# One ring of five PSUM banks and row-paired maxima products in an attention and feed-forward layer

## Chip, core and metric

One core of a Trainium2 chip runs the whole layer in one launch. The metric is the device time of a launch in microseconds (us); lower is better. The engines are TensorE (PE, with its weight loads as PEld), VectorE (DVE), ScalarE (ACT) and GpSimd (POOL); SyncE (SP) issues most of the DMAs. Each engine has its own written-out instruction stream, and semaphores alone order the streams against each other.

## What is computed

Input x and a context c, each 32 batches of 128 channels by 512 positions. Cut to what matters:

```python
x = x + xattn(layernorm(x), c)           # 8 heads of 16 channels, over 512 x 512 positions
x = x + ffn(layernorm(x))
# xattn: q = rope(Wq x + bq), k = rope(Wk c + bk), v = Wv c + bv
#        softmax(q k^T / 4) v, then Wo and bo
# ffn:   gate = bitlinear(x, w_gate); up = bitlinear(x, w_up)     (512 -> 2048)
#        y = fwht(silu(gate) * up); out = bitlinear(y, w_down)    (2048 -> 512)
# bitlinear: activations quantised to 8 bits by their row's absolute maximum, weights ternary
```

The softmax subtracts a maximum for each query. Any number near the true maximum serves, since it cancels between numerator and denominator.

## The kernel before

The work of one batch is spread over several steps. `step(t)` on every engine works on parts of batches t+2 to t-4 at once, and `for t in range(FIRST, LAST)` runs the steps. Inside `step` each engine's order is written out by hand, one call per piece of work, so an engine that waits holds back everything listed behind it.

Attention for a batch goes so:

- `project` makes q and k (f32, 128x512 each). DVE multiplies them with sine and cosine tables (`rope_sin`, `rope_cos`), SP moves the rotated half (`shift`, 2 DMAs), POOL adds (`turn`). Rows (channels) are ordered by channel first, then head, so that the rotated channels are the first 64 partitions.
- The result is cut into three bf16 parts whose sum is the f32 value: ACT makes part one and two (`first_part`, `second_part`), POOL the rests (`rest`, `third_part`). SP stacks them (`stack_part`, L314 to L329): 12 DMAs a batch write six blocks of 16 rows into `q_stack` and `k_stack`, in the pairings of `Q_TERMS` and `K_TERMS`, so that one product over 96 rows gives q k^T nearly to f32.
- `score_max` (L446 to L455): 32 products a batch, 96 rows deep, 128 queries by 512 keys, alternately into two banks `s1`. DVE takes each one's row maximum (`reduce_scores`, L1035). `max_transpose` turns the 128x32 maxima (L466), ACT negates them, and `stack_max` writes them as row 96 of `q_stack` by one DMA.
- `scores` (L470 to L481): 32 products again, now keys by queries and 97 rows deep, so that the maximum is already subtracted, alternately into two banks `s2`. ACT takes the exponential (`exps`, L726).
- `weigh` (L483 to L497): 8 groups a batch of four products each with v, 17 columns of weights for each head; the four write 32-partition strips of the bank `pv` side by side. In f32 the trace counts two instructions for each product, 8 in a group.
- After groups 3 and 7, `normalise` (L1037) transposes `pv` on DVE and takes the reciprocal of the sums; POOL multiplies (`mix`, L1314); after the second half DVE transposes back (`turn_back`), and `attn_out` is the product with Wo (L504).

Then the feed-forward part: `residual`, norm and quantisation on DVE and ACT; `gate_rows` (L522) and `xq_transpose` (L512); `gate_up` (8 groups of 16 products, L536) with `half_gates`, `tanh`, `glu` as consumers; the Walsh-Hadamard transform partly on POOL (`butterfly`) and partly as products (`hadamard`, L550); `y_transpose` (L561) and `down` (L574).

PSUM has eight banks: two `s1`, two `s2`, `pv`, and a ring of three. The names in `RING` take the ring's banks in turn in the order of the list, which is PE's order: `begin` waits until the bank's user before has been read, `end` tells that it is full.

Of the kernel before, what the change touches and what calls it, by code (L numbers as in the profile page):

```python
# [12 lines left out]
NH, DH = 8, 16  # L13
# [17 lines left out]
RING = {"yT0": 4, "yT1": 4, "down": 4, "wo": 2, "v": 0, "y0": 3, "mT": 1, "y1": 3, "y2": 3, "y3": 3, "hg": 2,  # L31
        "xqT": 2, "gate0": 2, "up0": 2, "gate1": 2, "up1": 2, "q": -1, "k": -1, "gate2": 2, "up2": 2, "gate3": 2,
        "up3": 2}
NRING = 3
# [5 lines left out]
FIRST, LAST = -6, B + 5  # L40

# [48 lines left out]
def layer(nc, x, ctx_in, proj_t, table_t, late_t, wg_t, wu_t, wd_t, out):  # L90
    stack = ExitStack()
    with stack:
# [83 lines left out]
        s1 = [stack.enter_context(nc.psum_tensor(f"s1_{i}", [128, 512], F32)) for i in range(2)]  # L176
# [42 lines left out]
        s1_full, s1_max = [sem(f"s1_full{i}") for i in range(2)], [sem(f"s1_max{i}") for i in range(2)]  # L219
# [77 lines left out]
        def _(sp):  # L297
# [16 lines left out]
            def stack_part(b, part):  # L314
                if not live(b):
                    return
                k = slot(b)
                sp.wait_ge((part1, part2, part3)[part], b + 1)
                sp.nop(nofuse=True)
                if part == 0:  # L320
                    wait(sp, s2_full, 32 * (b - 2))
                    sp.nop(nofuse=True)
                    if b < 3:
                        sp.wait_ge(ones_rows_set, b + 1)
                        sp.nop(nofuse=True)
                for w, (terms, dst) in enumerate(((Q_TERMS, q_stack[k]), (K_TERMS, k_stack[k]))):
                    for r in range(len(terms)):
                        if terms[r] == part:
                            sp.dma_start(dst[DH * r:DH * (r + 1), :, :], parts[:, part, w, :]).then_inc(stacked, 16)  # L329
# [14 lines left out]
            def stack_max(b):  # L344
# [4 lines left out]
                sp.dma_start(q_stack[slot(b)][STACK:STACK + 1, :, :], neg_max[:, :]).then_inc(max_stacked, 16)  # L349
# [20 lines left out]
            def step(t):  # L370
                load_late_consts(t + 1)
                load(t + 2)
                stack_max(t - 1)
                shift(t + 1)
                load_residual(t - 1)
                stack_part(t + 1, 0)
                stack_part(t + 1, 1)
                store(t - 4)
                stack_part(t + 1, 2)
                load_consts(t + 3)  # L380
# [7 lines left out]
        def _(pe):  # L388
# [57 lines left out]
            def score_max(b, n):  # L446
                if not live(b):
                    return
                k, p, i = slot(b), n % 2, n // 2
                h, c = 2 * (i // KC) + p, i % KC  # L450
                if n == 0:
                    pe.wait_ge(stacked, 16 * STACK_DMAS * (b + 1))
                wait(pe, s1_max[p], 16 * b + i)
                pe.matmul(s1[p][:, :], q_stack[k][0:STACK, h, 128 * c:128 * (c + 1)],  # L454
                          k_stack[k][0:STACK, h, :], start=True, stop=True).then_inc(s1_full[p], 1)  # L455

            def max_transpose(b):
# [5 lines left out]
                for p in range(2):  # L463
                    pe.wait_ge(s1_max[p], 16 * (b + 1))
# [5 lines left out]
            def scores(b, n):  # L470
# [4 lines left out]
                if n == 0:  # L475
                    pe.wait_ge(max_stacked, 16 * (b + 1))
# [3 lines left out]
                pe.matmul(s2[n % 2][:, :], k_stack[k][0:STACK + 1, h, 128 * c:128 * (c + 1)],  # L480
                          q_stack[k][0:STACK + 1, h, :], start=True, stop=True).then_inc(s2_full, 1)  # L481
# [96 lines left out]
            def step(t):  # L578
                bias_product(t)
                scores(t - 2, 19)  # L580
                score_max(t - 1, 16)
                weigh(t - 2, 3)
                score_max(t - 1, 17)
                scores(t - 2, 20)
                score_max(t - 1, 18)
                scores(t - 2, 21)
                y_transpose(t - 4, 0)
                score_max(t - 1, 19)
                scores(t - 2, 22)
                scores(t - 2, 23)  # L590
                score_max(t - 1, 20)
                weigh(t - 2, 4)
                scores(t - 2, 24)
                scores(t - 2, 25)
                score_max(t - 1, 21)
                score_max(t - 1, 22)
                weigh(t - 2, 5)
                score_max(t - 1, 23)
                scores(t - 2, 26)
                score_max(t - 1, 24)  # L600
                scores(t - 2, 27)
                y_transpose(t - 4, 1)
                score_max(t - 1, 25)
                scores(t - 2, 28)
                scores(t - 2, 29)
                score_max(t - 1, 26)
                down(t - 4, 0, 4)
                scores(t - 2, 30)
                up_sum(t - 1)
                score_max(t - 1, 27)  # L610
                score_max(t - 1, 28)
                scores(t - 2, 31)
                weigh(t - 2, 6)
                weigh(t - 2, 7)
                down(t - 4, 4, 8)
                score_max(t - 1, 29)
                score_max(t - 1, 30)
                down(t - 4, 8, 12)
                down(t - 4, 12, 16)
                score_max(t - 1, 31)  # L620
                attn_out(t - 2)
                project_v(t)
                hadamard(t - 3, 0)
                max_transpose(t - 1)
                score_max(t, 0)
                score_max(t, 1)
                hadamard(t - 3, 1)
                score_max(t, 2)
                hadamard(t - 3, 2)
                hadamard(t - 3, 3)  # L630
                score_max(t, 3)
                gate_rows(t - 2)
                xq_transpose(t - 2)
                scores(t - 1, 0)
                score_max(t, 4)
                scores(t - 1, 1)
                gate_up(t - 2, "gate", 0)
                gate_up(t - 2, "up", 0)
                scores(t - 1, 2)
                scores(t - 1, 3)  # L640
                gate_up(t - 2, "gate", 1)
                scores(t - 1, 4)
                gate_up(t - 2, "up", 1)
                scores(t - 1, 5)
                weigh(t - 1, 0)
                scores(t - 1, 6)
                scores(t - 1, 7)
                score_max(t, 5)
                project(t + 1, "q")
                score_max(t, 6)  # L650
                scores(t - 1, 8)
                score_max(t, 7)
                project(t + 1, "k")
                gate_up(t - 2, "gate", 2)
                scores(t - 1, 9)
                scores(t - 1, 10)
                score_max(t, 8)
                score_max(t, 9)
                weigh(t - 1, 1)
                scores(t - 1, 11)  # L660
                score_max(t, 10)
                scores(t - 1, 12)
                score_max(t, 11)
                gate_up(t - 2, "up", 2)
                scores(t - 1, 13)
                scores(t - 1, 14)
                gate_up(t - 2, "gate", 3)
                scores(t - 1, 15)
                score_max(t, 12)
                scores(t - 1, 16)  # L670
                weigh(t - 1, 2)
                score_max(t, 13)
                score_max(t, 14)
                scores(t - 1, 17)
                gate_up(t - 2, "up", 3)
                gate_sum(t + 1)
                score_max(t, 15)
                scores(t - 1, 18)
# [6 lines left out]
        def _(act):  # L685
# [169 lines left out]
            def max_out(b):  # L855
                if not live(b):
                    return
                wait(act, max_stacked, 16 * b)
# [4 lines left out]
            def step(t):  # L863
                norm1_apply(t + 1)
                exps(t - 1, 2)
                sign_piece(t - 2, 2, 4)
                exps(t - 1, 3)
                tanh(t - 2, 0)
                exps(t - 1, 4)
                tanh(t - 2, 1)  # L870
                exps(t - 1, 5)
                load_weights(t, 1, 1)
                abs_piece(t + 1, 0, 0)
                round_y(t - 3, 0)
                sign_piece(t - 2, 2, 5)
                abs_piece(t - 1, 2, 1)
                load_weights(t + 3, 0, 0)
                exps(t - 1, 6)
                exps(t - 1, 7)
                abs_piece(t - 1, 2, 2)  # L880
                exps(t - 1, 8)
                below_top(t - 3, 0)
                exps(t - 1, 9)
                exps(t - 1, 10)
                sign_piece(t - 2, 2, 6)
                round_y(t - 3, 1)
                sign_piece(t - 1, 1, 3)
                exps(t - 1, 11)
                abs_piece(t + 1, 0, 1)
                exps(t - 1, 12)  # L890
                exps(t - 1, 13)
                sign_piece(t, 0, 1)
                exps(t - 1, 14)
                sign_piece(t, 0, 2)
                abs_piece(t - 1, 2, 3)
                exps(t - 1, 15)
                tanh(t - 2, 2)
                abs_piece(t, 1, 0)
                abs_piece(t - 1, 2, 4)
                tanh(t - 2, 3)  # L900
                exps(t - 1, 16)
                abs_piece(t, 1, 1)
# [4 lines left out]
                below_top(t - 3, 1)  # L907
                exps(t - 1, 20)
                exps(t - 1, 21)
                exps(t - 1, 22)  # L910
                abs_piece(t + 1, 0, 2)
                exps(t - 1, 23)
                yT_out(t - 3, 0)
                abs_piece(t - 1, 2, 5)
                exps(t - 1, 24)
                second_part(t + 1)
                abs_piece(t + 1, 0, 3)
# [497 lines left out]
```

## Time and profile before

| what | value |
|---|---|
| median of 3 runs | 1508.82 us (1507.08 to 1510.89) |
| profiled execution | 1509.78 us, its span 1508.0 us |
| PE busy | 1414.5 us, 94% of the span |
| DVE busy | 1229.5 us, 82% |
| ACT busy | 1168.6 us, 77% |
| POOL busy | 1069.9 us, 71% |
| HBM over the span | 31 GB/s |

A matmul's busy time in the trace is longer than the time after which the next can start, since matmuls are pipelined: distances between starts say what PE can do. The chain of waits is followed back from the last instruction, and the durations in its pieces are such distances. The time before about 200 us is the loading and rounding of the weights and the filling of the pipeline; from about 1400 us the pipeline empties.

### The profile page before, as it was taken

To read this page: it belongs to the slowest core of one execution; us is meant where nothing else is said; L and a number is where in the kernel's file an instruction comes from. 1 tells how busy PE (TensorE), PEld (TensorE's weight loads), DVE (VectorE), ACT (ScalarE), POOL (GpSimd) and SP (SyncE) were. 2 spreads that over 40 slices of the span, in tenths; PEclk is the share of its full clock that TensorE was granted. 3 is DMA by queue.
4 is the path that set the end of the run, shared out by engine and by line. 5 is a ranking of instruction groups with operands and counts; after the bars stand their busy time and mean duration, and the time that the engine had idled before them with its cause. 6 is when DMAs were issued, how large, how long until landed. Compare 5 with 4: busy or idle time off the path is not lost.

```text
span 1508.0 us, 31029 instructions
## 1 busy us (share of the span) xinstructions
PE 1414.5 (94%) x11042; PEld 743.4 (49%) x11042; DVE 1229.5 (82%) x2149; ACT 1168.6 (77%) x2033; POOL 1069.9 (71%) x803
## 2 busy tenths in 40 slices
PE   2678999999999999999999999999999999999985
PEld 1214455455555544555555445555555455555443
DVE  2757788888888888888888888988888888888744
ACT  4586778888788888887788788877887888877663
POOL 3122788777777788777777887777778877777662
PEclk9677999999999999999999999999999999999998
DMA  8852344333344443323434433323344433333000
GB/s 211 225 116 46 58 72 77 62 65 62 61 74 68 78 78 64 66 62 60 77 64 78 78 64 71 60 64 69 64 78 78 72 64 63 64 52 64 16 8 15
DMA packets 81113, 108.13 MB, mean 72 GB/s; under 512 B 9664, under 2 KB 59200, under 8 KB 79936
## 3 DMA queue, kind: packets, MB, share of 16 engines
q1 hardware_dynamic: 77744, 93.56, 34.6%
q10 hardware_dynamic: 3216, 12.58, 2.4%
q8 instruction: 89, 1.46, 0.5%
q14 instruction: 64, 0.52, 0.2%
HBM read 38.73 MB, written 8.39 MB: 31 GB/s over the span
## 4 chain that ended last, share of the span: by engine, by line
PE 79%; ACT 9%; DVE 4%; DMA 3%; issue 3%; SPq 1%; POOL 1%; POOLq 0%; ACTq 0%; DVEq 0%
PE pv L495 15%; PE ring L536 14%; PE s L480 13%; PE s L454 13%; PE ring L574 7%; PE ring L550 6%; PE ring L428 4%; ACT region L726 4%; PE ring L504 2%; PE ring L442 2%; DMA region<-parts 2%; PE ring L561 1%; ACT parts L821 1%; ACT xqT L735 1%; ACT y_last L769 1%
## 5 line engine op out<-in xcount | busy, mean ns | idle before, releaser
L1035 DVE TENSOR_REDUCE maxima<-s 128x1 bf16<-128x512 f32 x1024 | 671.1, 683 | 110.4 <-PE s L454 107.8
L726 ACT ACTIVATE region<-s 128x512 f32<-128x512 f32 x1024 | 570.4, 594 | 101.0 <-PE s L480 93.0
L454 PE MATMUL s<-region 96*128 96x512 bf16 x1024 | 369.3, 390 | 26.2 <-DVE maxima L1035 13.5
L1293 POOL TENSOR_TENSOR region<-region,th 128x512 f32<-128x512 f32 x126 | 158.9, 1273 | 293.8 <-DVE th L1130 292.1
L480 PE MATMUL s<-region 97*128 97x512 bf16 x1024 | 357.8, 384 | 7.6 <-ACT region L726 4.0
L495 PE MATMUL pv<-region,v_ext 128*17 128x512 f32 x2048 | 264.2, 599 | 0.0
L292 POOL TENSOR_TENSOR region<-region 128x512 f32<-128x512 f32 x189 | 240.6, 1273 | 12.5
L293 POOL TENSOR_TENSOR region<-region 128x512 f32<-128x512 f32 x189 | 241.1, 1275 | 0.0
L454 PEld LDWEIGHTS s<-region 96*128 96x128 bf16 x1024 | 95.0, 98 | 207.3 <-DVE maxima L1035 110.9
L480 PEld LDWEIGHTS s<-region 97*128 97x128 bf16 x1024 | 91.0, 98 | 172.7 <-ACT region L726 140.0
L290 POOL TENSOR_TENSOR region<-region 128x1024 f32<-128x1024 f32 x63 | 148.0, 2371 | 3.4 <-DVE region L293 3.4
L536 PEld LDWEIGHTS ring<-xqT,wg 128*128 128x128 bf16 x2048 | 123.3, 98 | 52.6 <-issue 33.7
L536 PE MATMUL ring<-xqT,wg 128*128 128x128 bf16 x2048 | 135.8, 219 | 6.5 <-ACT xqT L735 1.7
L550 PE MATMUL ring<-late_const,region 128*128 128x128 f32 x1024 | 131.5, 277 | 7.5 <-POOL region L290 5.6
L536 PE MATMUL ring<-xqT,wu 128*128 128x128 bf16 x2048 | 135.3, 219 | 0.1
L550 PEld LDWEIGHTS ring<-late_const,region 128*128 128x128 f32 x1024 | 127.7, 194 | 15.1 <-issue 5.7
L536 PEld LDWEIGHTS ring<-xqT,wu 128*128 128x128 bf16 x2048 | 123.7, 98 | 15.2 <-DVE region L1121 0.3
L574 PE MATMUL ring<-wd,y_last 128*128 128x512 bf16 x512 | 128.1, 385 | 0.8 <-ACT y_last L787 0.8
L1121 DVE TENSOR_TENSOR region<-ring,half_gate 128x512 f32<-128x512 f32 x128 | 87.5, 684 | 41.8 <-PE ring L536 41.2
L836 ACT ACTIVATE v_ext<-ring 128x512 f32<-128x512 f32 x32 | 19.1, 598 | 126.9 <-PE ring L442 126.9
L1331 POOL TENSOR_TENSOR region<-region,rope_c 64x1024 f32<-64x1024 f32 x32 | 75.6, 2362 | 29.6 <-DMA rope_c<-region 27.4
L495 PEld LDWEIGHTS pv<-region,v_ext 128*17 128x17 f32 x2048 | 36.9, 95 | 109.8 <-issue 75.1
(111 smaller groups left out, 1862.5 us busy)
## 6 DMA issues: line engine op xcount, KB each, us to landing
region<-parts SPq DMA_DIRECT2D x384, 128.0 KB, 4.3
x_in<-in_x SPq DMA_DIRECT2D x32, 256.0 KB, 2.7
c_in<-in_ctx SPq DMA_DIRECT2D x32, 256.0 KB, 3.0
rope_c<-region SPq DMA_DIRECT2D x64, 128.0 KB, 2.3
x_res<-in_x SPq DMA_DIRECT2D x32, 256.0 KB, 2.9
out<-o_sb SPq DMA_DIRECT2D x32, 256.0 KB, 4.7
region<-in_wg_t ACTq DMA_DIRECT2D x1, 2048.0 KB, 8.9
region<-in_wu_t ACTq DMA_DIRECT2D x1, 2048.0 KB, 7.6
```

Of the source, the lines that this page charges most:

```text
L290: return engine.tensor_tensor(o[:, :, half, :], a[:, :, 0, :], a[:, :, 1, :], ALU.subtract if half else ALU.add)
L292: engine.tensor_tensor(o[:, :, 0, :], a[:, :, 0, :], a[:, :, 1, :], ALU.add)
L293: return engine.tensor_tensor(o[:, :, 1, :], a[:, :, 0, :], a[:, :, 1, :], ALU.subtract)
L454: pe.matmul(s1[p][:, :], q_stack[k][0:STACK, h, 128 * c:128 * (c + 1)], k_stack[k][0:STACK, h, :], start=True, stop=True).then_inc(s1_full ...
L480: pe.matmul(s2[n % 2][:, :], k_stack[k][0:STACK + 1, h, 128 * c:128 * (c + 1)], q_stack[k][0:STACK + 1, h, :], start=True, stop=True).then ...
L495: last = pe.matmul(pv[32 * i:32 * i + DH + 1, :], v_ext[b % 2][:, c, 4 * g + i, :], probs[:, (4 * u + i) % 8, :], start=(c == 0), stop=(c ...
L536: last = pe.matmul(bank(f"{name}{j}")[:, 128 * i:128 * (i + 1)], w[:, c, o:o + 128], xqT[:, c, :], start=(c == 0), stop=(c == HC - 1), ski ...
L550: last = pe.matmul(bank(f"y{j}")[:, 128 * c:128 * (c + 1)], z[:, o:o + 128], had[:, :], start=True, stop=True, skip_group_check=True)
L574: last = pe.matmul(bank("down")[:, :], yqT[:, c, :], wd[:, c, :], start=(c == 0), stop=(c == IC - 1))
L726: act.activation(probs[:, n % 8, :], s2[n % 2][:, :], ACT.Exp, scale=SCALE).then_inc(exp_done, 1)
L1035: dve.reduce_max(maxima[:, c, h:h + 1], s1[p][:, :], AXX).then_inc(s1_max[p], 1)
L1293: pool.tensor_tensor(zj, zj, th[:, j % 2, :], ALU.mult).then_inc(glu_done, 1)
```

## The change

1. **Ring.** `s1` is gone; the ring has five banks and takes the maxima products too, as `m0` to `m31`. `s2` and `pv` stay as they are. `RING` follows the new order of PE.
2. **Rows.** Channels are now ordered so that heads 0 to 3 lie in partitions 0 to 63 and heads 4 to 7 in 64 to 127 (with the rotated channels in every second block of 16). The stacks of the two head groups lie at different rows: terms 0 to 3 at rows 0 to 63 and 64 to 127. Terms 4 and 5 of the second group lie at rows 32 to 63, its row of maxima at row 31, and rows 0 to 30 of `q_stack` are set to zero once.
3. **Maxima products.** `score_max` issues two products, one of each head group, over the four main terms alone: 64 rows each, rows 0 to 63 and rows 64 to 127, into two ring banks. 16 such pairs a batch stand for the 32 products of before. The two smallest terms are left out of the maxima, not of the scores.
4. **Scores.** The products of heads 4 to 7 are 128 rows deep where they were 97.
5. **DMAs.** Every stacking DMA is cut in two by head group (24 a batch for 12), so is the one of the maxima (2 for 1); `shift` has 4 for 2, and `rope_sin` and `turn` work on 128 partitions for 64.
6. **Mix** goes from POOL to DVE, into `normalise`.
7. **Orders** of PE, ACT, DVE and SP are written anew, with the start of a step at another place.

```diff
-STACK_DMAS = 2 * len(Q_TERMS)
-SHIFTS = 2
-RING = {"yT0": 4, "yT1": 4, "down": 4, "wo": 2, "v": 0, "y0": 3, "mT": 1, ...
-NRING = 3
+STACK_DMAS = 4 * len(Q_TERMS)
+SHIFTS = 4
+RING = {"k": -1, "m4": 0, "m5": 0, "m6": 0, "m7": 0, "m8": 0, "m9": 0, "up2": 2, "m10": 0, "m11": 0, "gate3": 2,
+        "m12": 0, "m13": 0, "m14": 0, "m15": 0, "up3": 2, "m16": 0, "m17": 0, "m18": 0, "m19": 0, "yT0": 3, "m20":
+        0, "m21": 0, "m22": 0, "m23": 0, "m24": 0, "m25": 0, "m26": 0, "m27": 0, "m28": 0, "m29": 0, "m30": 0,
+        "m31": 0, "down": 3, "yT1": 3, "mT": 0, "wo": 1, "v": -1, "y0": 2, "y1": 2, "y2": 2, "m0": -1, "m1": -1,
+        "y3": 2, "hg": 1, "xqT": 1, "gate0": 1, "up0": 1, "gate1": 1, "q": -2, "up1": 1, "gate2": 1, "m2": -1, "m3":
+        -1}
+NRING = 5
+MAX_ROW = (STACK, 31)
+ROWS = (slice(0, STACK + 1), slice(0, 128))
+MAIN = (slice(0, 4 * DH), slice(4 * DH, 8 * DH))
+HALF = NH // 2
+def term_rows(g, r):
+    lo = DH * r if g == 0 else 64 + DH * r if r < 4 else 32 + DH * (r - 4)
+    return slice(lo, lo + DH)
+def heads(g):
+    return slice(HALF * g, HALF * (g + 1))
...
             def step(t):       # SP, the new order
+                stack_part(t, 2)
+                load(t + 2)
+                store(t - 4)
+                load_residual(t - 1)
+                load_consts(t + 3)
+                shift(t + 1)
+                load_late_consts(t + 1)
+                stack_part(t + 1, 0)
+                stack_part(t + 1, 1)
+                stack_max(t)
...
-            def score_max(b, n):
...
-                wait(pe, s1_max[p], 16 * b + i)
-                pe.matmul(s1[p][:, :], q_stack[k][0:STACK, h, 128 * c:128 * (c + 1)],
-                          k_stack[k][0:STACK, h, :], start=True, stop=True).then_inc(s1_full[p], 1)
+            def score_max(b, i):
...
+                k, c = slot(b), i % KC
+                if i == 0:
+                    pe.wait_ge(stacked, 16 * STACK_DMAS * (b + 1))
+                for g in range(2):
+                    begin(f"m{2 * i + g}", b)
+                for g in range(2):
+                    h = HALF * g + i // KC
+                    end(f"m{2 * i + g}",
+                        pe.matmul(bank(f"m{2 * i + g}")[:, :], q_stack[k][MAIN[g], h, 128 * c:128 * (c + 1)],
+                                  k_stack[k][MAIN[g], h, :], start=True, stop=True))
...
+                rows = ROWS[h // HALF]
+                pe.matmul(s2[n % 2][:, :], k_stack[k][rows, h, 128 * c:128 * (c + 1)], q_stack[k][rows, h, :],
+                          start=True, stop=True).then_inc(s2_full, 1)
...
-                dve.wait_ge(s1_full[p], 16 * b + i + 1)
-                dve.reduce_max(maxima[:, c, h:h + 1], s1[p][:, :], AXX).then_inc(s1_max[p], 1)
+                full(dve, f"m{n}", b)
+                free(f"m{n}", dve.reduce_max(maxima[:, c, h:h + 1], bank(f"m{n}")[:, :], AXX))
...
                 dve.reciprocal(inv_sum[:, :], blocks[:, :, DH]).then_inc(inv_done, 1)
+                dve.wait_ge(inv_done, 2 * b + g + 1)
+                if g == 0:
+                    wait(dve, attn_done, b)
+                dve.tensor_tensor(mixed[:, :].rearrange("p (n g e) -> p n g e", g=2, e=DH)[:, :, g, :],
+                                  blocks[:, :, 0:DH], inv_sum[:, :].unsqueeze(2).to_broadcast([128, 16, DH]),
+                                  ALU.mult).then_inc(mixed_done, 1)
```

PE's new order, written short (sc = `scores`, M = `score_max`, one pair each, W = `weigh`; a plus marks the batch one later): project k+; W0; sc 8, 9; M2; W1; M3; sc 10; M4; sc 11; up 2; sc 12; M5; sc 13; gate 3; sc 14, 15; M6; W2; M7; sc 16, 17; up 3; sc 18, 19; M8; W3; sc 20, 21; M9; y_transpose 0; sc 22, 23; W4; M10; sc 24, 25; M11, M12; sc 26, 27; W5; sc 28, 29; M13; W6; sc 30; M14, M15; sc 31; down (4 products); y_transpose 1; W7; max_transpose; down (12); attn_out; project_v; sc+ 0; hadamard 0; sc+ 1; hadamard 1, 2; M+ 0; hadamard 3; gate_rows; sc+ 2; xq_transpose; sc+ 3; gate 0; up 0; sc+ 4; gate 1; sc+ 5; project q; up 1; sc+ 6; gate 2; sc+ 7; M+ 1.

On ACT, `first_part` stands behind `exps` 17 as before, `second_part` behind `exps` 27 (it stood behind 24), and `max_out` behind the second `yT_out`. On DVE, maxima 23 to 31, `normalise` 1 and `turn_back` stand ahead of `residual`, and `quantise` between maximum 1 and the first `half_gates`. POOL keeps its order, without `mix`.

## Rows read from the trace of the kernel before

**Rows 1.** The page, part 1: busy us (share), instructions, by engine.
```profile
PE 1414.5 (94%) x11042; PEld 743.4 (49%) x11042; DVE 1229.5 (82%) x2149; ACT 1168.6 (77%) x2033; POOL 1069.9 (71%) x803
```

**Rows 2.** Stretches: span, busy of PE, PEld, DVE, ACT, POOL, PEclk, DMA, GB/s.
```profile
500.00:700.00 200.00, 198.92 (x1600) 106.37 (x1600) 173.60 (x309) 161.89 (x290) 153.34 (x115) 1.00 0.40 71
700.00:900.00 200.00, 199.16 (x1592) 102.73 (x1589) 174.55 (x305) 165.41 (x292) 160.67 (x121) 1.00 0.40 70
```

**Rows 3.** Chain of waits, 765 to 819 us: start, us to the next piece, what.
```profile
765.02 0.45 PE ring L561 x8
...
773.29 1.03 PE ring L504 x2
...
809.02 0.22 PE s L454
809.24 0.86 PE ring L574 x4
...
810.32 0.43 PE s L454 x2
...
810.97 1.84 PE pv L495 x16
...
816.16 1.02 PE ring L504 x2
...
818.97 0.32 PE ring L466 x4
819.29 0.54 PE s L454 x2
```

**Rows 4.** The same chain around one single group of weigh, then at xqT.
```profile
803.97 0.98 PE pv L495 x8
804.96 0.54 PE s L480 x2
...
823.78 0.60 ACT xqT L735
824.38 0.14 issue
824.52 1.95 PE ring L536 x32
```

**Rows 5.** Groups by line, 700 to 1000 us: count | busy us, mean ns | idle before.
```profile
L454 PEld LDWEIGHTS s<-region 96*128 96x128 bf16 x224 | 20.7, 97 | 35.4 <-DVE maxima L1035 16.8 <-issue 6.0
L1321 POOL TENSOR_TENSOR mixed<-turned_pv,inv_sum 128x256 f32<-128x256 f32 x14 | 8.7, 621 | 0.5
L1130 DVE SCALAR_TENSOR_TENSOR th<-th,ring 128x512 f32<-128x512 f32 x28 | 19.1, 682 | 0.4
L1099 DVE TENSOR_SCALAR gate_diag<-late_const,sc,w_half 128x128 f32<-128x128 f32 x7 | 2.4, 336 | 0.0
L821 ACT ACTIVATE parts<-region 128x1024 bf16<-128x1024 f32 x7 | 7.4, 1057 | 0.0
```

**Rows 6.** PE in order of time: start, us, what, count.
```profile
800.09 0.38 PE L454 MATMUL s<-region 96*128 96x512 bf16 x1
...
816.09 1.10 PE L504 MATMUL ring<-attn,late_const 128*128 128x512 f32 x2
819.22 0.61 PE L454 MATMUL s<-region 96*128 96x512 bf16 x2
```

**Rows 7.** DVE and ACT in order of time, attention's end to quantised x.
```profile
817.33 0.75 DVE L1066 SCALAR_TENSOR_TENSOR h_res<-ring,out_bias,x_res 128x512 f32<-128x512 f32 x1
822.69 0.43 DVE L1107 TENSOR_SCALAR xq<-turned_pv 128x512 bf16<-128x512 f32 x1
842.16 1.06 ACT L821 ACTIVATE parts<-region 128x1024 bf16<-128x1024 f32 x1
```

**Rows 8.** POOL and SP's queue in order of time: start, us to the last issue's end.
```profile
812.11 2.14 POOL L1344 TENSOR_TENSOR parts<-rope_c,parts 128x1024 bf16<-128x1024 f32 x1
814.32 1.19 SPq L329 DMA_DIRECT2D region<-parts  x2
821.07 0.72 SPq L349 DMA_DIRECT2D region<-neg_max  x1
843.36 4.08 SPq L329 DMA_DIRECT2D region<-parts  x6
```

**Rows 9.** DMA issues of 814 to 816 us: KB each, us to landing.
```profile
region<-parts SPq DMA_DIRECT2D x2, 128.0 KB, 3.4
```

More of the change, by code:

```diff
@@ L593, in step @@
[L593 to L627, printed above, removed]
+                project(t + 1, "k")
+                weigh(t - 1, 0)
+                scores(t - 1, 8)
+                scores(t - 1, 9)
                 score_max(t, 2)
-                hadamard(t - 3, 2)
-                hadamard(t - 3, 3)
+                weigh(t - 1, 1)
@@ L631, in step @@
                 score_max(t, 3)
-                gate_rows(t - 2)
-                xq_transpose(t - 2)
-                scores(t - 1, 0)
+                scores(t - 1, 10)
                 score_max(t, 4)
[L636 to L647, printed above, removed]
+                scores(t - 1, 11)
+                gate_up(t - 2, "up", 2)
+                scores(t - 1, 12)
                 score_max(t, 5)
-                project(t + 1, "q")
+                scores(t - 1, 13)
+                gate_up(t - 2, "gate", 3)
+                scores(t - 1, 14)
+                scores(t - 1, 15)
                 score_max(t, 6)
-                scores(t - 1, 8)
+                gate_sum(t + 1)
@@ L652, in step @@
+                weigh(t - 1, 2)
                 score_max(t, 7)
[L653 to L665, printed above, removed]
@@ new lines, in step @@
+                scores(t - 1, 19)
+                score_max(t, 8)
+                weigh(t - 1, 3)
+                scores(t - 1, 20)
+                scores(t - 1, 21)
+                score_max(t, 9)
+                y_transpose(t - 3, 0)
+                scores(t - 1, 22)
+                scores(t - 1, 23)
+                weigh(t - 1, 4)
+                score_max(t, 10)
+                scores(t - 1, 24)
+                scores(t - 1, 25)
+                score_max(t, 11)
+                score_max(t, 12)
@@ new lines, in step @@
+                scores(t - 1, 26)
+                scores(t - 1, 27)
+                weigh(t - 1, 5)
+                scores(t - 1, 28)
+                scores(t - 1, 29)
+                score_max(t, 13)
+                weigh(t - 1, 6)
+                scores(t - 1, 30)
+                score_max(t, 14)
+                score_max(t, 15)
+                scores(t - 1, 31)
+                down(t - 3, 0, 4)
+                y_transpose(t - 3, 1)
+                weigh(t - 1, 7)
+                max_transpose(t)
@@ new lines, in step @@
+                up_sum(t)
+                down(t - 3, 4, 8)
+                down(t - 3, 8, 12)
+                down(t - 3, 12, 16)
+                attn_out(t - 1)
+                project_v(t + 1)
+                scores(t, 0)
+                hadamard(t - 2, 0)
+                scores(t, 1)
+                hadamard(t - 2, 1)
+                hadamard(t - 2, 2)
+                score_max(t + 1, 0)
+                hadamard(t - 2, 3)
+                gate_rows(t - 1)
+                scores(t, 2)
@@ L680, in _ @@
+                xq_transpose(t - 1)
+                scores(t, 3)
+                gate_up(t - 1, "gate", 0)
+                gate_up(t - 1, "up", 0)
+                scores(t, 4)
+                gate_up(t - 1, "gate", 1)
+                scores(t, 5)
+                project(t + 2, "q")
+                gate_up(t - 1, "up", 1)
+                scores(t, 6)
+                gate_up(t - 1, "gate", 2)
+                scores(t, 7)
+                score_max(t + 1, 1)
             for t in range(FIRST, LAST):
@@ L1374, in _layout @@
     half = ROPE // 2
-    rows = [(d, h) for d in range(DH) for h in range(NH)]
+    order = [d for q in (0, 2, 1, 3) for d in range(half * q, half * (q + 1))]
+    rows = [(d, h) for g in range(2) for d in order for h in range(HALF * g, HALF * (g + 1))]
     perm = np.array([DH * h + d for d, h in rows])
```

269 lines of the change are left out of this document (112 added, 157 removed).

## The prediction

> **What bounds the kernel now.** I read the engines' totals first [rows 1]: PE 94%, DVE 82%, ACT 77%, POOL 71%. A PE share says little by itself, so the table of stretches comes next [rows 2]: in the steady part PE is busy 99.6% of the time (199.16 of 200 us) at full granted clock, DVE 87%, ACT 83%, POOL 80%. Third, the chain of waits: the two pieces of L504 (`attn_out`) stand 816.16 - 773.29 = 42.87 us apart, and nearly all pieces between them are PE's own [rows 3]. So a batch costs 42.87 us, 32 batches 1372 us, and the other 136 us of the span are weights, filling and emptying. PE's instruction distances are the bound.
>
> Those distances: one score product 0.22 us, two 0.43, so 0.218 each [rows 3]. One group of `weigh` takes 0.98, two adjacent ones 1.84, so a group is 0.86 and 0.12 more goes once for an excursion; the two score products right behind it take 0.54 instead of 0.43, another 0.11 [rows 3, 4]. The same shows without any four-fold packing: the four transposes of the maxima (8 columns of weights) take 0.32 where eight full transposes take 0.45, that is 0.10 too much, and the two products behind them again take 0.54 [rows 3]. I read this as the price of changing the shape in which the array is used: about 0.11 us for every change, the length of a weight load (97 ns [rows 5]) that isn't hidden. In PE's order of before there are 16 changes a batch (seven excursions to `weigh`, one to `max_transpose`).
>
> The Trainium skill says the same of the cause: TensorEngine Tiling (Array Packing), section Key Properties, has it that changing the tiling mode, not just the tile, drains the engine. The rows agree for column tiles at 0.11 us; no row shows a row tile. By that rule the isolated pairs would be nearly worthless, which is what I cost below.
>
> **The change, part by part.** *Maxima products.* 32 products of 0.218 go: 6.98 us a batch. 16 pairs come. If the two halves of the array run side by side, a pair takes 0.218 plus the offset of the second. That offset isn't in the trace: from 0 (four `weigh` products in 0.86 us leave nearly none) to 0.10 (a whole weight load [rows 5]). I take 0.03, nearer to `weigh`: 16 x 0.248 = 3.97. Saved: 3.0 us a batch; bounds 1.9 to 3.5.
>
> *Changes of shape.* I counted them in PE's new order, a pair as a third shape: 37 a batch, because only M11/M12 and M14/M15 are adjacent, and seven borders lie directly between a pair and a `weigh`. That is 21 more. At 0.11: +2.3 us. Bounds: 21 borders lie between pairs and full-array products alone; if a row pair changes for free, the others are 16, as before, and the term is 0. On the other side 0.16 each (L454's duration of 0.38 us [rows 6] less its distance of 0.218) would give 21 x 0.16 = 3.4. I take 2.3, since two kinds of change in the trace have one price.
>
> The net on PE is 3.0 - 2.3 = 0.7 us less a batch. Deeper scores (128 rows for 97) cost nothing: four 128-row products of `down` take 0.86, 0.215 each, as 96 rows do [rows 3].
>
> *From attention's end to the gates.* L504 starts at 816.09, DVE's residual at 817.33, the quantised x at 822.69, xqT is copied out from 823.78, and gates start at 824.52 [rows 4, 6, 7]: 8.4 us, of which PE waits about 0.7 (0.60 copy and 0.14 issue behind a transpose). In the new order PE has between the two: attn_out 1.0, v 0.9, four hadamards 3.6, four scores 0.9, one pair 0.45 with its changes, gate_rows 0.4, transposes 0.3 = 7.5 us. The same as before (one pair and four scores stand where six single products, one score and max_transpose stood). One DVE maximum between residual and absmax is gone, 0.3 us off that chain at best. I take no change; bounds -0.3 to +0.5.
>
> *Mix on DVE.* The 128x256 product of two SBUF operands isn't on DVE in the trace. Below, 0.34 (128x128, L1099); above, 0.68 (128x512, L1130) [rows 5]; I take 0.45 and 0.1 for the wait behind the reciprocal: 2 x 0.55 = 1.1 us. DVE then has 174.55/200 x 42.87 = 37.4, plus 1.1 = 38.5 of 42.2 us. It hides as long as PE's batch is over about 40 us. On the path to attn_out it replaces 0.62 us on POOL and a hand-over [rows 5]; from W7's end the chain is transpose, reciprocal, mix, transpose, some 2.4 us, and PE has max_transpose and twelve of `down` (2.9 us) to cover it. POOL gets 1.2 us shorter: nothing, it had slack. Wider `rope_sin` and `turn`: more partitions, same columns, nothing.
>
> *Ring.* With five banks PE waits for the fifth user back. Going down the new order with DVE at 0.6 to 0.65 us a maximum I find each bank free before its next user: closest are M12 and M15 (within 0.3 us) and max_transpose, which waits for maximum 31. Before, single maxima products also waited now and then (16.8 us in 300, on the weight load's row [rows 5]), with little effect on PE. I take 0; bounds -0.3 to +0.8.
>
> *DMAs.* A stacking issue takes SP 0.6 to 0.68 us (six in 4.08, two in 1.19), though the 8 KB of the maxima takes 0.72 [rows 8]: the size hardly matters, so cut DMAs cost their number. SP goes from 12 x 0.65 to 24 x 0.65 = 15.6 us, and about 22 us in all: no bound by itself. But the path matters: first_part ends 843.22 [rows 7]; then come 12 + 8 issues (13.0), two of maxima (1.4) and, because `stack_part(t, 2)` now stands behind `stack_max`, the last four (2.6); with the last one's landing (3.4 from its issue [rows 9], so 2.8 more) that is 19.8 us. The product that waits for it, M+ 0, is due at 819.22 + 42.87 = 862.09 in the old order [rows 6], 18.9 us after first_part, and in the new one 1.9 later (two hadamards and two scores more ahead of it, max_transpose less): 20.8. Waits for second_part and max_out on the way are worth 0 to 2 us. So it arrives between 1.0 early and 1.0 late. Halved DMAs should land sooner than 3.4; I take 0; upper bound 1.2.
>
> *Sum.* 32 x 0.7 = 22 us off the profiled execution's 1509.8 (span 1508.0 and 1.8 around it) is 1487; filling and emptying I leave alone, +-8. The median of before is 1 us under that execution. I say **1488**.
>
> **Rivals.**
> *B, row changes are cheap.* The 21 borders of pairs with full products cost nothing: PE would be 3.0 shorter, 39.9, and DVE with 38.5 and its own waits becomes the joint bound; I give 40.5: 32 x 2.4 = 77 off, 1433. For it: no row shows that a row pair drains the array. Against: two kinds of change cost the same.
> The page TensorE: Matmul & The Clock Gate of the Trainium skill, section Part 3: Packing small matmuls, says that weight loads overlap running matmuls when the row groups differ. No run here shows it; it would speak for B.
>
> *C, the last stacking DMAs come late* (slower). M+ 0 waits at SP's queue; PE and everything behind it, gate_rows and the quantised x too, shift by the lateness, so nothing absorbs it. At 1.2 us late the net is +0.5 a batch: 1526. It decides from 0.7 us late. For it: 26 issues in one row on SP, the path has no more than 1 us of air. Against: smaller DMAs. A ring wait of 1.2 us would read the same in time.
>
> *D, the pairs don't overlap* (or their price is far higher): 3.5 comes back, 32 x 2.5 = 80 more, 1590. Against: four column tiles of `weigh` clearly overlap.
>
> *E, nothing left:* offset 0.06 and 0.12 a change: within 5 us of 1509.
>
> **How the numbers follow.** Forecast 0.44 (its own range 1472 to 1504), B 0.16, C 0.25, D 0.04, E 0.11. A tenth of the forecast's cases fall within 0.3% (4.5 us, what measuring can tell from no change), some of C's too. Faster 0.57, same 0.13, slower 0.30. The range reaches from B to C: 1428 to 1534.
>
> **What would show it.** The batch distance of L504 falls to about 42.2 us. From the start of a full product ahead of an isolated pair to the start of the one behind it about 0.69 us; near 0.47 instead means B. Adjacent pairs (M11, M12) about 0.25 each. PE stays over 98% busy in the steady stretch, DVE near 91%. `mixed` on DVE 0.4 to 0.5 us, its wait for PE not longer than before. No wait of L454's line on the stacking DMAs; 0.7 us or more a batch there is C. Wrong would I be if the chain shows ACT or DVE as its largest owner, or if PE's weight loads wait for ring banks over 1 us a batch.

## The result, and the profile after

The changed kernel takes 1549.68 us (median of 4 runs, 1546.31 to 1551.89) against 1509.86 us: ratio 1.026, 95% interval 1.023 to 1.029. It is 2.6% slower where I forecast 1.4% faster. The profiled execution took 1546.31 us, span 1544.5 us.

The page after: span, totals by engine, the owners of the chain, and three of its groups (count | busy us, mean ns | idle before).

```profile
span 1544.5 us, 32084 instructions
...
PE 1372.3 (89%) x11042; PEld 692.7 (45%) x11042; DVE 1325.6 (86%) x2213; ACT 1178.1 (76%) x2033; POOL 1050.6 (68%) x742
...
DVE 44%; PE 38%; issue 7%; ACT 7%; SPq 1%; DMA 1%; POOL 1%; ACTq 0%; DVEq 0%; POOLq 0%
...
L1049 DVE TENSOR_REDUCE maxima<-ring 128x1 bf16<-128x512 f32 x1024 | 638.6, 682 | 23.4 <-PE ring L482 23.0
...
L482 PE MATMUL ring<-region 64*128 64x512 bf16 x1024 | 197.9, 392 | 34.6 <-DVE maxima L1049 27.8
...
L1066 DVE TENSOR_TENSOR mixed<-turned_pv,inv_sum 128x256 f32<-128x256 f32 x64 | 111.4, 1741 | 2.2
```

PE fell from 94% to 89% busy [rows 1], and the chain of waits, 79% PE's before, belongs to DVE for 44%, which I had named as a sign of being wrong. The last line is the finding: mix on VectorE lasts 1.74 us on average where I had taken 0.45. The stretch that answers to [rows 2] (span, busy of PE, PEld, DVE, ACT, POOL, PEclk, DMA, GB/s):

```profile
700.00:900.00 200.00, 188.16 (x1567) 97.89 (x1565) 182.86 (x310) 157.60 (x279) 142.72 (x103) 1.00 0.24 74
```

PE is busy 94.1% instead of 99.6, at the same full clock; DVE 91.4% instead of 87.3.

The chain of waits around attention's end (start, us, what), to be held against [rows 3, 4]:

```profile
785.26 1.03 PE pv L525 x8
786.32 0.73 DVE turned_pv L1059
787.07 0.27 DVE inv_sum L1062
787.36 2.06 DVE mixed L1066
789.46 0.05 issue
789.51 0.72 DVE attn L1075
790.23 0.14 issue
790.36 1.11 PE ring L534 x2
...
834.57 1.11 PE ring L534 x2
```

The two pieces of `attn_out` are 44.21 us apart (42.87 before). Between W7 and `attn_out` no PE piece stands in the chain: the twelve products of `down` are over, and PE waits for `attn`. The list of waits over 300 us, seven batches, has it first, and a second wait at the maxima products (engine, line waited for: us in total, times, longest):

```profile
PE ring L534 <- DVE attn L1075: 7.9, 7, 1.1
PE ring L482 <- DVE maxima L1049: 4.3, 13, 0.4
```


What holds the mix shows when DVE's rows are laid beside POOL's (start, us, engine, what). First a mix while POOL is idle, in the filling of the pipeline, then the two of one batch:

```profile
113.16 2.13 POOL L1355 TENSOR_TENSOR parts<-rope_c,parts 128x1024 bf16<-128x1024 f32 x1 [5.52 <-ACT parts L841]
...
118.31 0.42 DVE L1066 TENSOR_TENSOR mixed<-turned_pv,inv_sum 128x256 f32<-128x256 f32 x1
...
818.87 2.14 POOL L1349 TENSOR_TENSOR rope_c<-region,parts 128x1024 f32<-128x1024 f32 x1
819.68 1.60 DVE L1066 TENSOR_TENSOR mixed<-turned_pv,inv_sum 128x256 f32<-128x256 f32 x1
820.96 1.46 POOL L312 TENSOR_TENSOR region<-region 128x512 f32<-128x512 f32 x1
...
830.97 4.86 POOL L310 TENSOR_TENSOR region<-region 128x1024 f32<-128x1024 f32 x2
831.57 2.04 DVE L1066 TENSOR_TENSOR mixed<-turned_pv,inv_sum 128x256 f32<-128x256 f32 x1
```

Alone the mix takes 0.42. Beside L1349, which ends at 821.01, it ends at 821.28; beside the first half of the L310 pair it ends at 833.61, just after that instruction. Its recorded duration is mostly standing still. All 64 mixes of this trace say the same: one starts while POOL is idle and takes 0.42 us; the other 63 start during a POOL instruction, and each ends 0.28 us after that instruction's end. POOL pays too: L312 behind it takes 1.46 where it takes 1.27 otherwise. This reading is what the experiments put to the test.

### The profile page after: what moved, and what is told of

Its sections match the earlier page's. It is cut to its first block, busy times and chain, and to the rows that moved or that the text cites. A ratio compares the mean times of both kernels' runs of the same rounds, so it can differ in the third digit from the quotient of the medians.

```text
span 1544.5 us, 32084 instructions
## 1 busy us (share of the span) xinstructions
PE 1372.3 (89%) x11042; PEld 692.7 (45%) x11042; DVE 1325.6 (86%) x2213; ACT 1178.1 (76%) x2033; POOL 1050.6 (68%) x742
## 4 chain that ended last, share of the span: by engine, by line
DVE 44%; PE 38%; issue 7%; ACT 7%; SPq 1%; DMA 1%; POOL 1%; ACTq 0%; DVEq 0%; POOLq 0%
DVE maxima L1049 18%; PE ring L566 10%; DVE mixed L1066 7%; PE pv L525 7%; PE s L510 6%; PE ring L452 4%; PE ring L482 4%; DVE turned_pv L1059 3%; PE ring L534 2%; DVE th L1150 2%; PE ring L604 2%; DVE region L1029 2%; DVE attn L1075 1%; DVE region L1038 1%; DVE region L1141 1%
## 5 line engine op out<-in xcount | busy, mean ns | idle before, releaser
L740 ACT ACTIVATE region<-s 128x512 f32<-128x512 f32 x1024 | 570.3, 596 | 138.7 <-PE s L510 136.6
L1049 DVE TENSOR_REDUCE maxima<-ring 128x1 bf16<-128x512 f32 x1024 | 638.6, 682 | 23.4 <-PE ring L482 23.0
L510 PE MATMUL s<-region 128*128 128x512 bf16 (+1 forms) x1024 | 355.0, 387 | 9.5 <-DMA region<-neg_max 6.6
L525 PE MATMUL pv<-region,v_ext 128*17 128x512 f32 x2048 | 269.5, 598 | 1.6 <-ACT region L740 1.6
L312 POOL TENSOR_TENSOR region<-region 128x512 f32<-128x512 f32 x189 | 245.9, 1301 | 13.1 <-ACT wd L729 0.6
L313 POOL TENSOR_TENSOR region<-region 128x512 f32<-128x512 f32 x189 | 241.0, 1275 | 0.0
L482 PE MATMUL ring<-region 64*128 64x512 bf16 x1024 | 197.9, 392 | 34.6 <-DVE maxima L1049 27.8
L510 PEld LDWEIGHTS s<-region 128*128 128x128 bf16 (+1 forms) x1024 | 86.7, 97 | 205.0 <-ACT region L740 124.9
L310 POOL TENSOR_TENSOR region<-region 128x1024 f32<-128x1024 f32 x63 | 153.2, 2451 | 3.5 <-DVE region L313 3.4
L482 PEld LDWEIGHTS ring<-region 64*128 64x128 bf16 x1024 | 49.0, 93 | 233.6 <-issue 181.2
L1066 DVE TENSOR_TENSOR mixed<-turned_pv,inv_sum 128x256 f32<-128x256 f32 x64 | 111.4, 1741 | 2.2
L1342 POOL TENSOR_TENSOR region<-region,rope_c 128x1024 f32<-128x1024 f32 x32 | 75.5, 2360 | 40.6 <-DMA rope_c<-region 38.4
```

Source lines behind the costliest of these rows:

```text
L312: engine.tensor_tensor(o[:, :, 0, :], a[:, :, 0, :], a[:, :, 1, :], ALU.add)
L313: return engine.tensor_tensor(o[:, :, 1, :], a[:, :, 0, :], a[:, :, 1, :], ALU.subtract)
L482: pe.matmul(bank(f"m{2 * i + g}")[:, :], q_stack[k][MAIN[g], h, 128 * c:128 * (c + 1)], k_stack[k][MAIN[g], h, :], start=True, stop=True))
L510: pe.matmul(s2[n % 2][:, :], k_stack[k][rows, h, 128 * c:128 * (c + 1)], q_stack[k][rows, h, :], start=True, stop=True).then_inc(s2_full, 1)
L525: last = pe.matmul(pv[32 * i:32 * i + DH + 1, :], v_ext[b % 2][:, c, 4 * g + i, :], probs[:, (4 * u + i) % 8, :], start=(c == 0), stop=(c ...
L740: act.activation(probs[:, n % 8, :], s2[n % 2][:, :], ACT.Exp, scale=SCALE).then_inc(exp_done, 1)
```

## Experiments

Two theories were put to the test. Theory 1: a VectorE instruction with both inputs in SBUF doesn't run beside a GpSimd instruction that reads SBUF; the two mixes lost the time, everything else came out as forecast. Theory 2: row pairs, the ring or the cut DMAs lost it, and the mix only sits on the chain because PE is late. Every kernel ran beside the kernel before on the same chip (its median 1509 to 1511 us); not all ran on one chip, so a difference between two of them is uncertain by about 2 us more.

| kernel | us, median | ratio to before, 95% | batch distance us |
|---|---|---|---|
| kernel before | 1509.9 | | 42.92 |
| changed kernel | 1549.7 | 1.023 to 1.029 | 44.27 |
| mix_on_pool | 1501.8 | 0.993 to 0.996 | 42.64 |
| inverse_in_psum | 1492.2 | 0.987 to 0.990 | 42.34 |
| slow_first_half | 1520.9 | 1.005 to 1.009 | 43.40 |
| slow_second_half | 1541.6 | 1.019 to 1.023 | 44.17 |
| full_depth_maxima | 1518.3 | 1.004 to 1.008 | 43.23 |
| fewer_changes | 1519.4 | 1.005 to 1.008 | 43.22 |
| two_moves | 1497.8 | 0.991 to 0.994 | 42.56 |
| old_mix_dve | 1584.3 | 1.047 to 1.052 | 45.3 |
| old_mix_dve_psum | 1536.4 | 1.017 to 1.020 | 43.74 |
| old_extra_dve | 1514.2 | 1.001 to 1.004 | 43.00 |

The batch distance is worked out from the starts of the first and last `attn_out` products between 400 and 1300 us, as in this answer on its line in the changed kernel (min/median/max ns, first and last start us):

```profile
L534 PE MATMUL ring<-attn,late_const x40: 592/630/668, 436.6 to 1278.1; 128*128 128x512 f32 x40
```

Two instructions a batch, 0.43 us apart: (1278.1 - 0.43 - 436.6)/19 = 44.27. Where I say below how much a wait grew per batch, the distances between the starts of PE's products in the traces were summed by kind over the same 19 or 20 batches and compared between two kernels; such a sum also holds the part of a wait that lies within a product's recorded duration, which the lists of waits leave out.

**mix_on_pool**: the changed kernel, mix undone.

```diff
-                dve.tensor_tensor(mixed[...][:, :, g, :], blocks[:, :, 0:DH], inv_sum..., ALU.mult)   # in normalise
+                mix(t - 1, 0)          # POOL's step, L1321's code of before
                 third_part(t + 1)
+                mix(t - 1, 1)
```

> The changed kernel with one edit undone: mix goes back to GpSimd (the second half behind third_part, as in the kernel before). Theory 1 (the mix on VectorE is what cost the time: each of its 64 instructions lasts 1.7 us instead of 0.43 because it stands still while a GpSimd instruction runs, and it delays attn_out and loads VectorE): the batch distance of attn_out falls from 44.2 to 42.4-42.8 us, the time to 1485-1505 us; VectorE still waits for GpSimd between the halves since turn_back stands right behind normalise, which may cost up to 0.7 us a batch, 1520 at most. Theory 2 (the row pairs, the ring of five or the cut DMAs lose the time, the mix only sits on the chain because PE is late): the time stays at 1535-1550 us and attn_out moves little.

1501.8 us: theory 1's range, and theory 2's 1535 to 1550 is out. All else of the change is still in this kernel, and together it is faster than before.

**inverse_in_psum**: only the place of one operand of mix is changed, and with it what PE waits for before it writes `pv` again.

```diff
-        inv_sum = sb("inv_sum", [128, 16], F32)
+        inv_sum = pv[:, 0:16]
...
-                    wait(pe, pv_turned, 2 * b + g)
+                    wait(pe, mixed_done, 2 * b + g)
```

> The changed kernel with mix on VectorE as it is, but the 16 columns of inv_sum lie in PSUM (the first columns of the pv bank) instead of SBUF, and PE waits for mix instead of for the transpose before it writes pv again. Same instructions, same engine; only one operand's memory is changed. Theory 1 (a VectorE instruction with two SBUF inputs and a GpSimd instruction exclude each other): mixed takes 0.40-0.55 us in all of its 64 instructions, the batch distance is 42.3-42.6 us, the time 1482-1498 us, close to what I had forecast. Theory 1b (mix is slow by its strided and broadcast operands in the steady part): mixed stays at 1.6-2.0 us and the time at 1545. Theory 2 (pairs, ring, DMAs): mixed gets short, but the time stays over 1530 us.

1492.2 us, 1.1% faster than before (ratio 0.989, 0.987 to 0.990). The mix's own line, all 64 of them (min/median/max ns):

```profile
L1066 DVE TENSOR_TENSOR mixed<-turned_pv,pv x64: 420/420/421, 107.1 to 1433.0; 128x256 f32<-128x256 f32 x64
```

and the same line in the changed kernel:

```profile
L1066 DVE TENSOR_TENSOR mixed<-turned_pv,inv_sum x64: 425/1628/2487, 107.5 to 1487.0; 128x256 f32<-128x256 f32 x64
```

The strides and the broadcast are the same, so they aren't what was slow (theory 1b of the expectation falls). One of the two inputs moved from SBUF to PSUM, and every wait beside POOL is gone. The Trainium skill states it: SBUF — State Buffer, section Who interferes with whom, says that a DVE instruction with two SBUF inputs contends with a GpSimd instruction that reads SBUF, and that the port pair they share is an exclusive lock. The traces agree, 0.42 against up to 2.49 us.

The distances between PE's starts say where the changed kernel's 1.93 us a batch over this one lie: 1.31 in front of `attn_out`, 0.71 at M11 and M12, and 0.1 less elsewhere. So both waits come from the mix, and nothing of note is left over.

**slow_first_half, slow_second_half**: `inverse_in_psum` with the inverse of one half of the heads in SBUF again.

```diff
-        inv_sum = pv[:, 0:16]
+        inverse = [pv[:, 0:16], pv[:, 0:16]]
+        inverse[0] = sb("inv_sum", [128, 16], F32)      # the other kernel: inverse[1]
```

> As inverse_in_psum, but for the first half of the heads the inverse lies in SBUF again, so only the first mix of a batch can be held by GpSimd. Theory 1: the first mix takes 1.2-1.8 us, the second 0.42. It loads VectorE with about 1.2 us more a batch in a stretch where maxima follow one on another; in the changed kernel PE waited 0.65 us a batch at M11 and M12 behind it. Expected distance 42.6-43.1 us, time 1500-1520 us. Theory 2 (only the path to attn_out counts): no change from 1492 us.

> As inverse_in_psum, but for the second half of the heads the inverse lies in SBUF again. Theory 1: the second mix takes 1.7-2.1 us, stands between attention's last product and attn_out, and PE waits about 1.1 us there: distance 43.3-43.5 us, time 1522-1532 us. If the two halves add up, slow_first_half and slow_second_half together lose the 57 us between 1492 and 1549.

1520.9 and 1541.6 us: 29 and 49 us more, where both halves slow lose 57. They don't add, and both came out above their range. The second mixes (median here 2.42 us, 2.03 in the changed kernel, since they meet the GpSimd instruction earlier) make PE wait up to 1.5 us for `attn`, 1.7 a batch by the starts. For the first, the waits (over 300 us, as above) name a cause that the changed kernel doesn't have:

```profile
PEld pv L526 <- DVE mixed L1067: 9.0, 7, 1.3
PE pv L526 <- DVE mixed L1067: 6.9, 7, 1.0
```

In this family PE may write `pv` only after the mix, for the inverse lies in it, so a slow first mix holds W4: 1.06 us a batch by the starts, all that this kernel loses. M11 and M12, where the changed kernel waits, don't wait longer here. The two kernels therefore show that either slow mix can cost PE time, but not the shares of the changed kernel; those are the 1.31 and 0.71 above.

**full_depth_maxima**: `inverse_in_psum` with the pairs' products at full depth (`FULL`: rows 0 to 95 for heads 0 to 3, all 128 for heads 4 to 7), order and all else kept.

```diff
-                        pe.matmul(bank(f"m{2 * i + g}")[:, :], q_stack[k][MAIN[g], h, 128 * c:128 * (c + 1)],
-                                  k_stack[k][MAIN[g], h, :], start=True, stop=True))
+                        pe.matmul(bank(f"m{2 * i + g}")[:, :], q_stack[k][FULL[g], h, 128 * c:128 * (c + 1)],
+                                  k_stack[k][FULL[g], h, :], start=True, stop=True))
```

> As inverse_in_psum, but each maxima product runs over the full array's rows (96 for heads 0-3, 128 for heads 4-7, so row 31 with an old maximum shifts the maxima of heads 4-7: the numbers that come out are others) instead of a 64-row pair; orders, ring, DMAs and all else stay. Theory 1 with my costing (a pair takes 0.22 us, each change of shape 0.105-0.11): 32 x 0.218 for 16 x 0.22 is +3.5 us, 21 changes fewer is -2.3 us: +1.2 us a batch, 43.2-43.6 us, 1520-1533 us. If row changes were free (a pair then saves all of its 0.22): +3.5 us, 1590 or more. If pairs are worthless: 1485-1495 us.

1518.3 us, 0.9 us a batch more than with pairs: somewhat under the expected 1.2, the distance just inside its range (43.2 to 43.6) and the time just under. So the pairs are worth about 0.9 us a batch net, not the 3.5 that 16 hidden products would be. Here is where the rest goes, in the chain of `inverse_in_psum` (start, us to the next piece, what):

```profile
740.37 0.32 PE ring L482 x2
740.69 0.32 PE s L510
741.01 0.32 PE ring L482 x2
741.33 0.32 PE s L510
...
746.37 0.54 PE s L510 x2
...
757.97 0.54 PE ring L482 x4
```

A single product takes 0.22 [rows 3]; one ahead of a pair takes 0.32. A pair takes 0.22 + 0.10, two adjacent pairs (M14, M15) 0.54, so a pair itself costs as much as one product, its second half next to nothing (it starts 3 ns behind the first), and each change of shape 0.10, close to the price read off `weigh` [rows 3, 4]. From the product ahead of an isolated pair to the one behind it are 0.64 us, where I had named 0.69 for my forecast and 0.47 for rival B: the pair with its two changes takes 0.42, as long as two single products. Summed over a batch by the starts, `full_depth_maxima` spends 3.3 us more on the 16 products that a pair hides (3.5, less a wait of 0.2 at M12); the pairs' 21 borders with full products cost 2.0, the f32 products behind a pair 0.2, and 0.2 goes elsewhere: 0.9 is left.

**fewer_changes, two_moves**: pieces of PE's order moved so that changes go.

```diff
+                score_max(t, 4)            # both kernels: M4 behind M3
                 scores(t - 1, 10)
-                score_max(t, 4)
...
+                score_max(t, 9)            # both: M9 behind W3
                 scores(t - 1, 20)
                 scores(t - 1, 21)
-                score_max(t, 9)
...
-                weigh(t - 1, 5)            # fewer_changes only
                 scores(t - 1, 28)
                 scores(t - 1, 29)
+                weigh(t - 1, 5)
```

> As inverse_in_psum, with three moves in PE's order that leave the ring's order as it is: M4 directly behind M3, M9 directly behind W3, scores 28 and 29 ahead of W5 instead of behind it. 4 changes of shape a batch fewer. Theory 1 (PE bound, 0.105-0.11 us for each change): -0.43 us a batch, 41.85 us, 1476-1482 us. If the earlier pairs or scores run into a wait on VectorE's maxima or ScalarE's exponentials, less: up to 1492 us.

1519.4 us: a clear miss, 27 us slower than `inverse_in_psum` where I expected it faster. Its chain:

```profile
766.71 0.34 PE s L510
767.05 0.02 issue
767.07 1.09 ACT region L740 x2
768.17 0.05 issue
768.21 0.39 PE s L510
768.60 0.98 PE pv L525 x8
```

Scores 28 and 29 go into the two `s2` banks and wait for exponentials 26 and 27 (the piece L740 x2); W5 behind them starts late, and exponential 28 waits for it (ACT for PE, 0.6 us), since it writes the probability tile that W5 reads.

> As fewer_changes, without its third move (scores 28 and 29 stay behind W5): M4 directly behind M3, M9 directly behind W3, 3 changes of shape a batch fewer than inverse_in_psum. If fewer_changes was lost by its third move alone (scores 28 and 29 waited for exponentials 26 and 27, and exponential 28 for W5 to free its place in the 8 probability tiles), the distance is 42.28 - 0.32 = 41.96 us and the time 1480-1486 us. If the shorter PE order runs into VectorE or ScalarE anyway: 1488-1496 us.

1497.8 us, 0.4% slower than `inverse_in_psum` and not 0.6% faster, above both stated ranges: the second miss. Three changes went, and this came:

```profile
752.33 0.34 PE s L510
752.70 0.04 issue
752.75 1.09 ACT region L740 x2
753.84 0.05 issue
753.89 0.39 PE s L510
```

The scores after M9 come one pair later, so PE stands at the next of them until two exponentials are done. PE is 98% busy in this order and ACT empties its two score banks one after the other, so a move that saves 0.1 us for PE can cost more in a wait for ACT: counting changes alone doesn't price a move.

**old_mix_dve, old_mix_dve_psum, old_extra_dve**: the part done alone in the kernel before.

```diff
                 dve.reciprocal(inv_sum[:, :], blocks[:, :, DH]).then_inc(inv_done, 1)
+                dve.wait_ge(inv_done, 2 * b + g + 1)                       # the first two
+                ...
+                dve.tensor_tensor(mixed[...], blocks[:, :, 0:DH], inv_sum..., ALU.mult).then_inc(mixed_done, 1)
...
+                wait(dve, extra_done, 2 * b + g)                           # old_extra_dve instead
+                dve.reduce_max(scratch[:, :], table_const[:, 0:256], AXX).then_inc(extra_done, 1)
```

> The kernel before with mix alone moved to VectorE (both operands in SBUF): one part of the change done alone. Theory 1: mixed takes 1.2-2.5 us there too; VectorE has some 5.5 us of air in a batch, the two mixes take 2.6 us of it beyond their own price, and the second delays turn_back by up to 1 us, where PE has little cover: 1512-1535 us. If the mix had its own price of 0.43 us and nothing else, the time would stay at 1505-1512 us. Theory 2: 1505-1512 us whatever mixed takes.

1584.3 us, 4.9% slower, twice as much as the whole change and far over my range. The mix alone (mean 1.38 us) hits the old order harder: in 300 us of the steady part the maxima's weight loads waited 30.7 us for DVE's maxima (16.8 before [rows 5]), and `attn_out` up to 0.9 us. By the starts, PE lost 2.4 us a batch, 1.4 around the score and maxima products and 1.0 in front of `attn_out`.

> The kernel before with mix on VectorE and inv_sum in PSUM. Theory 1: mixed 0.40-0.55 us; time 1503-1512 us, no difference from before. Theory 1b: mixed as long as in the version with both operands in SBUF, and the same time as that.

1536.4 us where I expected 1503 to 1512, with mix at 0.42 us throughout. Theory 1's price for the mix held, its consequence here didn't. The waits show PE's next `weigh` behind the mix in all 7 batches:

```profile
PEld pv L495 <- DVE mixed L1052: 7.3, 7, 1.1
```

That is `pv`, released after reciprocal and mix instead of after the transpose. By the starts this holds the weigh groups 0.6 us a batch longer, and `attn_out` comes 0.2 later; together they are the 0.82 us by which the batch grew. `old_extra_dve` takes the same DVE time without that wait and without POOL:

> The kernel before, mix on GpSimd as it was, with one more VectorE instruction of about 0.41 us (a row maximum over 256 constant columns, one SBUF input, its result is not used) right behind each reciprocal: the load of a short mix on VectorE without mix's wait for GpSimd and without a later release of pv. If VectorE's load alone is harmless in the old order: 1506-1514 us, and the 27 us that old_mix_dve_psum lost come from PE waiting for mix before it may write pv (1.1 us a batch in its trace). If the load itself or the later maxima cost them: 1525-1540 us.

1514.2 us (ratio 1.002, 1.001 to 1.004): 0.4 us of DVE twice a batch costs nearly nothing, as I had costed it. So DVE's load isn't what cost the 27 us; some three quarters of them are the later release of `pv`, by the starts, though a kernel with that wait alone was not run. In the new order the same wait is 0.2 us a batch, which fits that the PSUM operand pays there and not here.

## Why the prediction was wrong

The step that failed is **Mix on DVE**: "I take 0.45 and 0.1 for the wait behind the reciprocal: 2 x 0.55 = 1.1 us" and "from W7's end the chain is transpose, reciprocal, mix, transpose, some 2.4 us". The bounds, 0.34 and 0.68, came from VectorE rows that each read one tensor from SBUF; mix reads two. Measured: 0.42 of its own, but 1.6 us beside `rest` and 2.03 us beside `butterfly`, 3.6 us a batch in place of 0.9. POOL is busy 80% of the steady part [rows 2], and 63 of the 64 mixes met one of its instructions. The chain from W7's end (786.32 to 790.36) is 4.0 us, and PE's cover of 2.9 us didn't reach: 1.3 us a batch by the starts. The same excess puts DVE behind in the run of maxima, and PE waits 0.7 us a batch longer at M11 and M12. Instead of hiding, the term cost 44.27 - 42.34 = 1.9 us a batch, 57 us in all; no rival of mine named it. I had weighed VectorE's load, not what its instruction shares with POOL's.

The other steps, one by one:

- *Maxima products.* 3.0 us forecast with 0.03 for the second half of a pair; the offset is 3 ns and the term 3.5, the upper bound.
- *Changes of shape.* 21 more at 0.11 = 2.3 forecast; 0.10 each, 2.0, and 0.2 more at the f32 products behind a pair, which I hadn't priced. Entering or leaving a row pair costs about the same as a column tile. Rival B (cheap row changes, 1433 us) is refuted by the pieces above, rival D (no overlap) as well.
- *Net on PE.* 42.2 us a batch forecast, 42.34 in `inverse_in_psum`; 1488 us forecast, 1492 measured there. With the mix's collision taken out, the sum holds within 0.3%. Part of that is luck: against `full_depth_maxima` the pairs bring 0.9 us a batch where 0.7 was forecast, and that kernel is 0.3 slower than the one before (43.23 against 42.92), so the new order itself cost 0.3 where I had put nothing. The next point has most of it.
- *From attention's end to the gates.* No change forecast; 8.2 us in the changed kernel (834.57 to 842.78) for 8.4 [rows 4, 6]. My inventory of the old order there was off (five single maxima products and two scores, not six and one), and what I concluded from it was wrong: seven single products (1.5 us) and `max_transpose` (0.3 and its two changes) are not "the same" as one pair and four scores (1.35), but 0.7 more. The chain over DVE and ACT kept its length, PE had less to do beside it, and so PE stands longer in front of the gates: 0.80 us a batch in the new order (in `inverse_in_psum` the last score starts at 771.06 and the gates at 772.08, less the 0.22 of the score), 0.30 in the old (824.00 to 824.52).
- *Ring.* No wait for a bank forecast. In the changed kernel there are waits (4.3 us in seven batches, by the list), at M11 and M12, behind the slow mix. With the inverse in PSUM the list over the same stretch has none, but M12 starts 0.40 us behind M11, where M15 starts 0.22 behind M14: 0.18 us a batch of waiting stay, at one of the places I had called closest.
- *DMAs, rival C.* No maxima product waits for the stacking DMAs in the steady part. A half-size issue takes 0.59 us at the median, the whole took 0.60, but it lands after 2.6 us at the median instead of 4.3: the last ones are in time. C had the sign right by another mechanism, which is no credit.

The range ended at 1534 us, since of the two slower rivals it took in only C.

## What to carry to other kernels

Before an element-wise instruction is moved from GpSimd to VectorE, look where its inputs lie: with two tensors in SBUF it takes turns with GpSimd, and when it ends is then set by GpSimd's instruction (here 0.28 us after its end); one input in PSUM frees it (0.42 us in all 64), if the bank's next writer can wait. Price array packing with its changes of shape, 0.10 us each here: an isolated pair (0.42 us) gains nothing over two full products (0.43), two adjacent pairs do (0.64 with both changes, for 0.87). And try a move in a packed order before counting it: three changes fewer made the kernel slower.

## What the runs showed beyond that

The best version of all is `inverse_in_psum`, 1492.2 us: 1.1% under the kernel before, 3.7% under the changed one. It differs from the latter by the place of 16 columns and the wait that goes with it. It is also 10 us faster than `mix_on_pool`, run beside it on the same chip: moving the mix to VectorE was worth having, once it no longer met GpSimd. Cutting the stacking DMAs in two by partitions left the time of one issue as it was, 0.59 us, and took the landing from 4.3 to 2.6 us (median), so a cut costs queue time and gives latency.
